# A four-layer block on one core: attention's second variance product, its residual sums, and the order of work in the two top-2 expert stages

## The reference, cut to what matters

```
router_probs = softmax(x @ router_w + router_b)
top_p, top_i = top_k(router_probs, 2);  top_p = top_p / sum(top_p)
expert_out = einsum('bnd,edc->bnec', x, expert_w) + expert_b
out = einsum('bnk,bnkc->bnc', top_p, gathered(expert_out, top_i))
```

## Time and profile before

| | us |
|---|---|
| median of 3 runs | 6848.14 (6845.38 to 6849.93) |
| the profiled execution, own time | 6859.88 |
| its span | 6858.1 |
| TensorE busy | 5320.3 (78%) |
| VectorE busy | 4319.6 (63%) |
| ScalarE busy | 3684.3 (54%) |
| GpSimd busy | 1269.2 (19%) |

### The profile page before, as it was taken

How to read it: one execution, slowest core, us unless ns; L and a number is a source line. 1 busy time by engine, 2 the same in 40 slices (tenths; PEclk the granted TensorE clock), 3 DMA queues, 4 the chain that set the end, 5 groups by cost and what they waited for, 6 DMA issues and landing times. The chain is left out here.

```text
span 6858.1 us, 132327 instructions
## 1 busy us (share of the span) xinstructions
PE 5320.3 (78%) x45758; PEld 3504.9 (51%) x45758; DVE 4319.6 (63%) x9710; ACT 3684.3 (54%) x6946; POOL 1269.2 (19%) x1164
## 2 busy tenths in 40 slices
PE   6776777644996777669996999614999999857777
PEld 4554555422553333349996999201555555423333
DVE  5665766779224777772222344878777777668776
ACT  4554555547444666462224322636677677656564
POOL 2333333215120000050000000032111112211110
PEclk9888888875997888869998999857999999978888
DMA  1111011223234777530000022425676666547766
GB/s 27 29 29 32 20 32 26 81 66 95 80 86 138 241 237 235 189 98 0 0 0 0 0 86 92 130 76 97 83 86 83 83 78 75 64 151 220 217 204 202
DMA packets 794230, 645.98 MB, mean 94 GB/s; under 512 B 496551, under 2 KB 644199, under 8 KB 793779
## 3 DMA queue, kind: packets, MB, share of 16 engines
q1 hardware_dynamic: 792755, 639.06, 37.9%
q0 software_dynamic: 1024, 1.05, 0.1%
HBM read 549.78 MB, written 90.20 MB: 93 GB/s over the span
## 5 line engine op out<-in xcount | busy, mean ns | idle before, releaser
L2343 PE MATMUL sw_pC<-sw_row,sw_wc 128*128 128x128 f32 x10160 | 1159.5, 274 | 56.1 <-DVE sw_row L2218 54.9
L2343 PEld LDWEIGHTS sw_pC<-sw_row,sw_wc 128*128 128x128 f32 x10160 | 1148.2, 191 | 58.2 <-DVE sw_row L2218 55.5
L2777 PE MATMUL sp_pC<-sp_work,sp_bands 64*64 64x512 f32 (+11 forms) x14592 | 985.7, 428 | 43.9 <-issue 43.9
L2206 DVE SCALAR_TENSOR_TENSOR sw_row<-sw_pC,sw_y 128x128 f32<-128x128 f32 x1016 | 337.3, 332 | 792.6 <-PE sw_pC L2343 792.6
L2777 PEld LDWEIGHTS sp_pC<-sp_work,sp_bands 64*64 64x64 f32 x14592 | 600.7, 133 | 432.2 <-issue 364.6
L2716 ACT ACTIVATE sp_pC<-sp_pC,sp_par 128x512 f32<-128x512 f32 x832 | 597.8, 741 | 371.8 <-PE sp_pC L2777 348.3
L1755 DVE TENSOR_TENSOR t_z<-t_z,t_ht 128x1024 f32<-128x1024 f32 x512 | 644.7, 1300 | 163.5 <-DMA t_z<-gate_rows 160.2
L2275 ACT ACTIVATE sw_y<-sw_row 128x128 f32 (+1 forms) x762 | 265.1, 348 | 593.5 <-DVE sw_row L2206 593.5
L1917 PE MATMUL t_pO<-t_z,t_ew 128*64 128x512 f32 x2048 | 554.3, 690 | 3.2 <-DVE t_z L1755 3.1
L2673 DVE TENSOR_TENSOR sp_work<-sp_work,sp_pC 128x512 f32<-128x512 f32 x512 | 351.3, 687 | 169.8 <-ACT sp_pC L2716 169.3
L1887 PE MATMUL t_pT<-t_ident,t_h 128*128 128x128 f32 x1024 | 194.5, 352 | 257.8 <-ACT t_gs L1814 153.6
(11 more groups left out here) (369 smaller groups left out, 10553.0 us busy)
## 6 DMA issues: line engine op xcount, KB each, us to landing
t_z<-gate_rows SPq DMA_DIRECT2D x512, 512.0 KB, 5.9
sp_bands<-windows SPq DMA_DIRECT2D x128, 512.0 KB
c_spent<-tokens SPq DMA_DIRECT2D x128, 256.0 KB, 2.6
cb_xs<-tokens SPq DMA_DIRECT2D x128, 256.0 KB, 2.8
wa_xs<-in_x SPq DMA_DIRECT2D x64, 256.0 KB, 2.8
tokens<-wa_xt SPq DMA_DIRECT2D x128, 128.0 KB, 2.3
tokens<-cb_h SPq DMA_DIRECT2D x64, 256.0 KB, 2.4
t_xs<-tokens SPq DMA_DIRECT2D x32, 512.0 KB, 9.2
```

The lines of the kernel that those rows point to most:

```text
L2206: dve.scalar_tensor_tensor(row[par][c][:, :, PAD:PAD + P2], pC[c][:, 0:2 * P2].rearrange("p (b w) -> p b w", b=2), 0.0, line(sweep, c, i), ...
L2343: ins = pe.matmul(pC[c][:, 0:2 * P2], wc[:, sweep, m, :], row[1 - par][c][:, :, m:m + P2], start=(m == 0), stop=(m == 4))
L2777: ins = pe.matmul(out[halves[to], :, low * lo:low * hi], band[halves[k], (NV * g + j) % BANDS, q, AT[k][tap], :], v[halves[k], :, low * at ...
```

## The change

In attention TensorE's `variance(n + 1, 1)` moves from the end of step 1 to step 2, behind `scores`; on GpSimd `residual(n - 1)` now stands ahead of `write_h(n + 1)`. In both top-2 stages the order of the beat is changed on VectorE, ScalarE and TensorE, and for t3 the column loads run two tiles further ahead.

```
 # attention, GpSimd
+                    if j == 2 and not first:
+                        residual(n - 1, (k - 1) % NX)
                     if j == 2 and not last:
                         write_h(n + 1, (k + 1) % 2, NSTEP * n)
-                    if j == 2 and not first:
-                        residual(n - 1, (k - 1) % NX)
 # attention, TensorE
                     scores(s)
+                    if j == 2 and not last:
+                        variance(n + 1, 1)
...
-                    if j == 1 and not last:
-                        variance(n + 1, 1)
 # top-2, SyncE (t3 alone)
                 spread_gates(0, i)
+                if rows is not None:
+                    load_columns(7 + i)
...
-                    load_columns(2 * n + 7)
+                    load_columns(2 * n + 9)
...
-                    load_columns(2 * n + 8)
+                    load_columns(2 * n + 10)
 # top-2, VectorE, beat n before
-    stats(n+2); weigh(n,0,[0]); route(n+1); weigh(n,0,[1]); norm(n+2)
-    weigh(n,0,[2]); gate(n+1); weigh(n,0,[3]); weigh(n,1,range(4))
 # top-2, VectorE, beat n after
+    weigh(n,0,[0,1]); gate(n+1); weigh(n,0,[2,3]); stats(n+3)
+    weigh(n,1,range(4)); route(n+2); norm(n+3)
 # top-2, ScalarE, beat n: root(n+3) one place up
-    save_mixed(n, 1); root(n+3)
+    root(n+3); save_mixed(n, 1)
 # top-2, TensorE, beat n, m = n+2
-    turn_gates(n+1); turn(m,0); mix(n,0); turn(m,1); route(m); mix(n,1)
+    mix(n,0) with turn_gates(n+1) behind its second pair
+    turn(m,0); turn(m,1); route(m); mix(n,1)
```

More of the change, by code:

```diff
@@ L1652, in _ @@
                     load(n + 4)
-                if rows is not None and 2 * n + 7 < 2 * NB:
-                    load_columns(2 * n + 7)
+                if rows is not None and 2 * n + 9 < 2 * NB:
+                    load_columns(2 * n + 9)
                 if n > 0:
@@ L1659, in _ @@
                     spread_gates(n + 1, 0)
-                if rows is not None and 2 * n + 8 < 2 * NB:
-                    load_columns(2 * n + 8)
+                if rows is not None and 2 * n + 10 < 2 * NB:
+                    load_columns(2 * n + 10)
                 if n + 1 < NB:
@@ L1757, in beat @@
             def beat(n):
[L1758 to L1768, removed]
+                weigh(n, 0, [0, 1])
+                if n.plus(1).within(NB):
                     gate(n.plus(1))
-                weigh(n, 0, [3])
+                weigh(n, 0, [2, 3])
+                if n.plus(3).within(NB):
+                    stats(n.plus(3))
                 weigh(n, 1, range(4))
+                if n.plus(2).within(NB):
+                    route(n.plus(2))
+                if n.plus(3).within(NB):
+                    norm(n.plus(3))
             first = Beat(0, 0, 0)
-            stats(first)
-            norm(first)
-            stats(first.plus(1))
+            for i in range(2):
+                stats(first.plus(i))
+                norm(first.plus(i))
+            stats(first.plus(2))
             route(first)
-            norm(first.plus(1))
+            norm(first.plus(2))
             gate(first)
+            route(first.plus(1))
             over_beats(dve, beat, link, 3 + 11 + 1 + 3)
@@ L1847, in beat @@
                         save_logits(m, i)
-                save_mixed(n, 1)
                 if n.plus(3).within(NB):
                     root(n.plus(3))
+                save_mixed(n, 1)
                 finish(n, 0)
@@ L1868, in _ @@
             root(first.plus(1))
+            root(first.plus(2))
             gap(first)
             prepare(first.plus(1), first)
-            root(first.plus(2))
             gap(first.plus(1))
@@ L1910, in turn_gates, with mix @@
                              ident[:, :]).then_inc(gates_turned, 1)
-            def mix(m, i):
+            def mix(m, i, gates_of=None):
                 since(pe, oc_saved, 2 * m.n + i - 1)
                 for q in range(4):
+                    if gates_of and q == 2:
+                        turn_gates(gates_of, 4 * m.n + 7)
                     pe.wait_ge(z_ready, 8 * m.n + 4 * i + q + 1)
@@ L1945, in beat @@
                 due = m.within(NB)
-                if n.plus(1).within(NB):
-                    turn_gates(n.plus(1), 4 * n.n + 7)
+                mix(n, 0, n.plus(1) if n.plus(1).within(NB) else None)
                 if due:
[L1949 to L1952, removed]
+                    for i in range(2):
+                        turn(m, i)
                     route(m)
```

## The result

| | before | after |
|---|---|---|
| median us | 6849.03 (6845.38 to 6851.96, 4 runs) | 6521.66 (6517.22 to 6523.44, 4 runs) |
| span of the profiled execution | 6858.1 | 6521.7 |
| attention, to the first instruction of the next stage | 1301.2 | 1143.3 |
| t1, from its first weight difference on VectorE to the first copy of the sweeps | 751.8 | 658.8 |
| t3, from its first weight difference to the end | 853.6 | 768.6 |

The ratio is 0.9521, 95% interval 0.9505 to 0.9538: 327 us less, where 248 were forecast. All of it lies in the three stages that the change touches: 157.9, 93.0 and 85.0 us of the spans' difference of 336.4.

The account below looks back on a forecast made before the run. No engine is full; waits closing rings of in-order engines bound the kernel. Attention -135, t1 -52 and t3 -61 us sum to -248: 6612 us for an execution like the profiled one, 6600 for the median; range 6505 to 6730.

Parts of the forecast that it names:

- The two waits of a strip: Attention, TensorE: 3.9 us for ScalarE's first logarithm and 3.4 us for GpSimd's residual sum, each about once a strip.
- The residual fits into GpSimd's idle time: Attention: the sum, 2.34 + 0.25 us, ends 2.4 us before `root` is done, so GpSimd's `write_h` is not later.
- The pair of `write_h`: Attention: VectorE's and GpSimd's copies start together; VectorE's takes 3.36 us beside GpSimd's, where it took 1.46 behind it.
- 4.7 us a strip: Attention: gain taken for each of 28 strips with both waits, 132 us; 135 us for the stage.
- more than forecast: Rival, 13%: TensorE keeps full clock through shorter waits; 6.3 us a strip, beats of 19.0 and 20.8 us; 6526 us.
- Ring one: Top-2 stages: ScalarE normalises, TensorE turns halves around `mix(n,0)`; 21.14 us a beat in t1 becomes 18.8, in t3 20.6.
- Ring two: Top-2, t1: gate, spread copy, VectorE's product, `route`, next gate; closes at 21.14 us, with 14.2 us left after the change.
- 21.8 us a beat in t3: T3: beat expected instead of 23.92 us, as VectorE is busy 20.12; 29 x 2.1 = 61 us saved.
- The column loads cost nothing and hide the sums: T3: loads two tiles ahead, so `stats(n+3)`, half a beat earlier, finds its tiles summed.
- `root` one place up costs nothing: Top-2 stages: `root` moved up is free because ScalarE idles there until `mix(n,1)` ends.
- The slower one: Rival, 4%: top-2 gate read-back latency grows from 10.7 to 19.9 us or more; at 22 us, 6968 us.

Follow-up runs that it names:

- `write_h` one by one: Changed kernel with GpSimd's `write_h` started only when VectorE's is done: 6493.59 us; a second one adds two constant TensorE products a strip: 6487.79 us.
- top-2 alone: Kernel before with the whole top-2 edit in both stages, column loads included, and attention as before: 6680.83 us, ratio 0.975.

## Why the prediction was right, and by how much it was off

The range held the time, and the sum was 24% too small. Step by step:

- *The two waits of a strip stand one behind the other.* Shown: 15 to 19 us for the variance move alone, 107 for the residual move, 160 together.
- *The residual fits into GpSimd's idle time.* Shown by the timeline: 416.86 to 420.34, `write_h` at 421.07. But it fits more closely than forecast: it takes 3.5 us, not 2.6, because the second sum, of 32 columns, takes 1.23 us beside VectorE's subtraction where 0.25 was assumed. Of 2.4 us to spare 0.7 are left.
- *The pair of `write_h` costs VectorE 3.36 us and lies on the path.* It took 3.50, and taking the clash away saved 28 us. The estimate in the sum, 0.9 us a strip, times 28 is 25.
- *4.7 us a strip.* Mis-sized: regular strips are 5.3 us shorter (37.6 to 32.3). The forecast left the variance product at its 2.05 us in every strip, where the mean is now 1.58 (1.95 before), and the transposes at 1.1 where they took 0.60. The "more than forecast" case named this cause and put it at 6.3. Beyond that, the strips at a turn of the hardware loop, 41.7 to 43.6 us before, are at 33.4 to 35.6; their excess over a regular strip shrank from 4.6 to 2.1 us, which I had not counted. The 22 regular strips and the four at a turn give 148 of the 158 us; the sum had 135 for all. Why the turn costs less was not tried. With `write_h` one by one the excess is back at 5.0.
- *Ring one in t1 becomes 18.8 us.* Shown: 18.60. Three kernels bear out that it is this ring which closes the beat: TensorE's order alone gives most of the gain, six VectorE instructions fewer give none, and a ScalarE instruction in another place moves the beat by 0.07 us. But I took 19.2, a little above VectorE's need. And I took the gain against a regular beat of 21.14, while the regular beats were 21.1, 21.3 and 22.5 in turn (`mix(n,0)`, inside the ring, took 4.2, 4.8 and 5.6 us where `mix(n,1)` took 3.65) and are now all 18.60. The mean beat went from 22.4 to 19.3, 3.1 us, where 1.9 stood in the sum: 93 us instead of 52.
- *Ring two is 21.1 us and closes at the same time.* Wrong, though it did no harm to the sum, because the change shortens both. TensorE's order alone gives 152.5 of 178 us with VectorE's old order. The latency from a gate to its product is real and went only from 11.3 to 10.2 us in the mean; the rest of the ring, `route` and the next gate, had waits for ScalarE and TensorE in it, which are ring one. That VectorE's order gives 14 us more in t1 once TensorE's is changed says that ring two then counts again.
- *21.8 us a beat in t3, nearer to VectorE's load than to the ring.* Mis-sized: many beats are at 20.4 to 20.6, the ring's own length as worked out there. The mean of all went from 24.7 to 22.0, 2.7 us against the 2.1 in the sum, and 31 of them make 83 of the 85 us. VectorE's load does not close this beat either, by the kernel with six instructions fewer. The sum of this stage has a slip as well: 61 less the 3 for the start and the 1 for each image's end is about 55, not 61.
- *The column loads cost nothing and hide the sums.* Shown; without them 41 us of t3 are lost.
- *`root` one place up costs nothing.* Right in sign: it gains 0.07 us a regular beat of t1. In the whole time it can't be seen.

Of the rivals, "more than forecast" was the nearest, 6526 against 6521.66. That it came so near is luck: it had 176 us for attention and 58 for t1, where 158 and 93 came. The slower one needed a gate latency of 19.9 us. The landing time of the spread copies did rise, at the median from 5.9 to 7.7 us, while VectorE's waits for them fell. They are not gone, as the prediction had it: behind the ends of two images in t3 VectorE still waits 7.6 and 7.9 us, and these beats last 28.3 and 28.1 us (30.5 and 30.3 before).

## What to carry to other kernels

Where two in-order engines wait for each other twice in a period, try both edits together and each on top of the other: the variance move gave 19 us alone and 53 on top of the residual move. A ring's length read off a trace may contain another ring's waits; before it is called a bound of its own, take out each wait in it that another ring causes. In this kernel two engines that block each other and are released by the same event were faster one after the other, by a wait.

## What the runs showed of the hardware that I had not expected

- With GpSimd's three instructions behind VectorE's instead of beside them, both take less: 1.36 and 2.64 us against 3.50 and 3.61. Together they cost 3.6 us, one after the other 4.2, so the pair loses little by it; VectorE gains 2.1.
- In the kernel before, with TensorE's first wait filled, the lower clock behind it was gone, but the stretch at the lower clock behind the next wait of 5 us grew from 3.0 to 6.4 us. The mean clock rose from 0.85 to 0.89 and the time did not fall.
- GpSimd's sum of 32 columns took 1.23 us beside VectorE's subtraction and 0.25 without it.
- T3 read 775.4 and 775.9 us in the two kernels with `write_h` one by one, against 768.6 and 768.9 in the changed kernel and with top-2 alone. Their t3 code is the same but for its place in the program. Each is one profiled execution, and the cause stays open.
